# Graph kernel on one core: count scatters among the key gathers, eight buffers for turned blocks, all attribute gathers beside the hops

## The reference, cut to what matters

```python
x = layernorm(x + L0(x))   # 2 transformer layers: attention over edges, then an FFN
x = layernorm(x + L1(x))   # GAT, 4 heads
x = layernorm(x + L2(x))   # hypergraph convolution, twice
x = layernorm(x + L3(x))   # messages from edge_attr_4 and a radial MLP of edge_attr_10

# L0, for each of two layers
scores = einsum('ehd,ehd->eh', q[dst], k[src]) * scale
agg = segment_sum(softmax_by_dst(scores) * v[src], dst)
# L2, for each of two convolutions
m = segment_sum(xt[src], dst) * Binv
out = segment_sum(m[dst], src) * Dinv
# L3
s = node_in[src]; messages = tensor_product(s, edge_attr_4) * radial
agg = segment_sum(messages, dst)
```

## Time and profile before

| | us |
|---|---|
| median of 3 runs | 5292.75 |
| lowest and highest | 5285.0, 5301.71 |
| profiled execution, its own time | 5281.95 |
| its span | 5280.8 |

### The profile page before, as it was taken

One profiled execution on the slowest core, in us unless ns is written; L12 is line 12 of the kernel. 1 busy time (PEld: TensorE's weight loads), 2 busy tenths in 40 slices (PEclk: granted clock), 3 DMA queues, 4 the chain that ended last, 5 costly groups with the idle time before them and its releaser, 6 DMA issues.

```text
span 5280.8 us, 60302 instructions
## 1 busy us (share of the span) xinstructions
PE 3594.7 (68%) x15291; PEld 2666.6 (50%) x15291; DVE 2872.9 (54%) x6726; ACT 1861.5 (35%) x5462; POOL 3684.8 (70%) x3085
## 2 busy tenths in 40 slices
PE   4544444566896444449979705666669999888886
PEld 3433323344564232336646503444458888677876
DVE  6455556888443454578864305666772223334445
ACT  1143334565333343447733201111120100256555
POOL 4466666888887666678888886666687887266664
PEclk9876667899998676669989857888789999889898
DMA  7688887566325898867743225666649899666665
GB/s 258 196 284 273 281 286 218 140 160 135 34 27 140 284 288 288 278 156 166 167 97 26 23 39 149 171 173 167 141 90 285 236 256 261 184 175 176 175 176 143
DMA packets 734946, 951.06 MB, mean 180 GB/s; under 512 B 277381, under 2 KB 526260, under 8 KB 734472
## 3 DMA queue, kind: packets, MB, share of 16 engines
q1 hardware_dynamic: 419634, 538.30, 33.2%
q0 software_dynamic: 298192, 385.84, 31.5%
q10 hardware_dynamic: 16774, 23.00, 1.2%
HBM read 727.03 MB, written 219.80 MB: 179 GB/s over the span
## 4 chain that ended last, share of the span: by engine, by line
PE 32%; issue 23%; DVE 18%; POOL 15%; another core or an unknown queue 5%; DMA 4%; ACT 2%; DVEq 1%; ACTq 0%; POOLq 0%; SPq 0%
PE bank L2657 11%; POOL arena L928 7%; POOL ATT L965 7%; PE bank L2782 6%; PE bank L2362 4%; PE bank L2779 4%; DMA ATT<-arena 3%; DVE arena L1371 3%; DVE arena L1473 2%; DVE arena L1383 2%; DVE arena L1753 2%; PE bank L2564 2%; PE bank L2575 2%; POOL arena L972 2%
## 5 line engine op out<-in xcount | busy, mean ns | idle before, releaser
L928 POOL DMA_INDIRECT arena<-KVT,arena x832 | 802.2, 964 | 479.2 <-issue 272.3
L2497 PE MATMUL bank<-arena 128*128 128x264 f32 x1664 | 600.5, 513 | 660.9 <-issue 322.3
L2497 PEld LDWEIGHTS bank<-arena 128*128 128x128 f32 x1664 | 385.8, 249 | 875.4 <-issue 619.8
L972 POOL DMA_INDIRECT arena<-ATTR,arena x416 | 660.9, 1589 | 155.7 <-issue 155.7
L965 POOL DMA_INDIRECT ATT<-arena x391 | 644.5, 1648 | 124.8 <-issue 109.2
L951 POOL DMA_INDIRECT sc<-arena x391 | 639.2, 1635 | 129.7 <-issue 111.8
L928 POOL DMA_INDIRECT arena<-YT,arena x416 | 406.3, 977 | 299.6 <-issue 105.9
L1473 DVE TENSOR_TENSOR arena<-arena,bank 128x256 f32<-128x256 f32 x832 | 297.2, 411 | 564.8 <-remote 368.1
L928 POOL DMA_INDIRECT arena<-X1T,arena x416 | 414.0, 995 | 249.0 <-issue 129.7
L2454 PE MATMUL bank<-arena 128*128 128x273 f32 x1664 | 454.1, 411 | 141.8 <-DVE arena L1532 94.8
L2270 ACT ACTIVATE arena<-arena 128x128 f32<-128x128 f32 x1248 | 374.9, 387 | 259.1 <-issue 133.4
(11 more groups left out here) (334 smaller groups left out, 6435.7 us busy)
## 6 DMA issues: line engine op xcount, KB each, us to landing
VE<-arena SPq DMA_DIRECT2D x208, 512.0 KB
arena<-VE SPq DMA_DIRECT2D x208, 512.0 KB
left<-ATT SPq DMA_DIRECT2D x250, 320.0 KB
left<-AM SPq DMA_DIRECT2D x250, 320.0 KB
ATT<-arena POOLq DMA_DIRECT2D x25, 1600.0 KB, 6.2
arena<-LOCT SPq DMA_DIRECT2D x312, 128.0 KB
arena<-ATT SPq DMA_DIRECT2D x75, 384.0 KB
AM<-arena SPq DMA_DIRECT2D x100, 256.0 KB
```

Source lines behind the costliest of these rows:

```text
L928: GP.indirect_dma_start(out=ring[:, i % n, k, :], out_offset=None, in_=table, in_offset=bass.IndirectOffsetOnAxis(ap=idx[:, 4 * i + k:4 * ...
L972: GP.indirect_dma_start(out=PA[:, c, 2:6], out_offset=None, in_=ATTR, in_offset=bass.IndirectOffsetOnAxis(ap=PA[:, c, 0:1].bitcast(I), axi ...
L2497: mm = P.matmul(b_[:, 0:264], OHQ[:, i % 3, k * 128:(k + 1) * 128], QS[:, i % 4, k, :], start=True, stop=True)
```

## The change

Three things change.

1. **Counts among the gathers.** A function `count(n)` issues one count scatter. In k0 and k1 one stands behind every second group's gathers, 52 in each stage, 104 in all. The other 287 stay behind k1's gathers. The waits for the places and for the cleared table move ahead of k0's first gather.
2. **Attributes.** The 52 early attribute gathers go; all 416 stand behind l1's gathers, beside the hops, with the wait for `attr_out`.
3. **Eight buffers for turned blocks.** AMT grows from four to eight buffers and moves to the region of the K/V ring (`o_big + 256`). The semaphores `am_out` are dropped; the stores of AM signal the eight semaphores `kept`, of which five are the former `v_kept`.

```diff
-EARLY = 52
+AMRING = 8
@@
-    AMT = view(o_S + 3584, 4, 4, 128)
+    AMT = view(o_big + 256, AMRING, 4, 128)
@@
-    v_kept = [Landed(nc, f"v_kept{k}") for k in range(5)]
+    kept = [Landed(nc, f"kept{k}") for k in range(AMRING)]
+
+    def am_kept(f):
+        k = f % AMRING
+        return kept[k]((2 * len(range(k, G, 5)) if k < 5 else 0) + f // AMRING + 1)
@@
-                                 AMT[:, f % 4, 0:nb, :]).then_inc(am_out[f % 4].sem, 16)
+                                 AMT[:, f % AMRING, 0:nb, :]).then_inc(kept[f % AMRING].sem, 16)
@@
+        def count(n):
+            g, k = n // 4, n % 4
+            c = g + KG * k
+            if g:
+                GP.wait_ge(*counted[k](g))
+            GP.indirect_dma_start(
+                out=ATT, out_offset=bass.IndirectOffsetOnAxis(ap=PLACE[:, c:c + 1], axis=0),
+                in_=ones[:, 0:1], in_offset=None, bounds_check=TABLE - 1,
+                compute_op=ALU.add).then_inc(counted[k].sem, 16)
+
         GP.wait_ge(*index_made("prep", 1))
+        GP.wait_ge(*edges_made("places", 1))
+        GP.wait_ge(*table_clear(PIECES + 1))
@@
-                    GP.wait_ge(*v_kept[i % 5](l * len(range(i % 5, G, 5)) + i // 5))
+                    GP.wait_ge(*kept[i % 5](l * len(range(i % 5, G, 5)) + i // 5))
                 gather(k_, i, KVT, 512, isrc, o_big)
+                if i % 2:
+                    count(l * (G // 2) + i // 2)
@@
-                GP.wait_ge(*edges_made("places", 1))
-                GP.wait_ge(*table_clear(PIECES + 1))
-                for g in range(KG):
-                    for k in range(4):
-                        c = g + KG * k
-                        if c < C:
-...
+                for n in range(2 * (G // 2), C):
+                    count(n)
@@
-        GP.wait_ge(*attr_out(1))
-        add_attributes(range(EARLY))
@@
-        add_attributes(range(EARLY, T))
+        GP.wait_ge(*attr_out(1))
+        for c in range(T):
+...
@@
-            if f >= 4:
-                S.wait_ge(*am_out[f % 4](f // 4))
-            S.activation(AMT[:, f % 4, 0:nb, :], bank[f % 2][:, 0:128 * nb].rearrange("p (b s) -> p b s", s=128),
+            if f >= AMRING:
+                S.wait_ge(*am_kept(f - AMRING))
+            S.activation(AMT[:, f % AMRING, 0:nb, :], bank[f % 2][:, 0:128 * nb].rearrange("p (b s) -> p b s", s=128),
                          ACT.Copy).then_inc(block_copied.sem, 1)
```

More of the change, by code:

```diff
@@ L323, in program @@
     COUNTS = view(o_S, 4, 896)
-    AMT = view(o_S + 3584, 4, 4, 128)
+    AMT = view(o_big + 256, AMRING, 4, 128)
+    assert 256 + AMRING * 512 <= o_ring - o_big
     RS1 = ACC[:, :, 256:260]
@@ L477, in program @@
     left_in = [Landed(nc, f"left_in{k}") for k in range(RIGHT)]
-    am_out = [Landed(nc, f"am_out{k}") for k in range(4)]
     y_out = [Landed(nc, f"y_out{k}") for k in range(4)]
@@ L647, in sync_engine @@
                 SY.wait_ge(*gathered(f"k{l}", i))
-                SY.dma_start(VE[i], KV[:, i % 5, :, 256:512]).then_inc(v_kept[i % 5].sem, 16)
+                SY.dma_start(VE[i], KV[:, i % 5, :, 256:512]).then_inc(kept[i % 5].sem, 16)
                 if i + 6 < G:
@@ L652, in sync_engine @@
             for k in range(5):
-                SY.wait_ge(*v_kept[k]((l + 1) * len(range(k, G, 5))))
+                SY.wait_ge(*kept[k]((l + 1) * len(range(k, G, 5))))
             def load_emb(n):
@@ L780, in sync_engine @@
             if h == 1:
-                for k in range(4):
-                    SY.wait_ge(*am_out[k](2 * W))
+                for f in range(8 * W - AMRING, 8 * W):
+                    SY.wait_ge(*am_kept(f))
             for part in range(5):
@@ L986, in pool_engine @@
             gather("l1", i, X1T, 72, idst, o_ring)
-        add_attributes(range(EARLY, T))
+        GP.wait_ge(*attr_out(1))
+        for c in range(T):
+            GP.indirect_dma_start(
+                out=PA[:, c, 2:6], out_offset=None, in_=ATTR,
+                in_offset=bass.IndirectOffsetOnAxis(ap=PA[:, c, 0:1].bitcast(I), axis=0), bounds_check=R1 - 1,
+                compute_op=ALU.add).then_inc(attr_back.sem, 16)
         GP.wait_ge(*acc_clear("l3", 1))
@@ L1790, in end1 @@
             yield from norm_windows("a0", part)
-        for k in range(4):
-            V.wait_ge(*am_out[k](2 * W))
+        for f in range(8 * W - AMRING, 8 * W):
+            V.wait_ge(*am_kept(f))
         V.wait_ge(*w_landed(W_LOADS["l2"]))
@@ L2081, in scalar_engine @@
             for k in range(5):
-                S.wait_ge(*v_kept[k]((l + 1) * len(range(k, G, 5))))
+                S.wait_ge(*kept[k]((l + 1) * len(range(k, G, 5))))
             copy_scan(f"w{l}", SPs)
```

## The result

The changed kernel took 5335.9 us (median of 4, 5332.35 to 5338.27) beside 5294.03 us for the kernel before (median of 4): ratio 1.0087, 95% interval 1.0074 to 1.0099. The forecast was 5225, the range 5140 to 5345; the time fell into the range's upper end, but the kernel got slower and not faster.

The account below looks back on a forecast made before the run. POOL was taken to bound the stretch before l1, by late counts and early attributes. From the profiled 5281.95 us, -116 + 30 + 0 + 18 gave 5214, plus 10.8 for the median 5225 us; 8-in-10 range 5140 to 5345.

Parts of the forecast that it names:

- additive rival: k0 and k1: ring waits don't shrink, so counts cost 193 us, not 30; 5388 us; chance 0.14 for cost past 114.
- term 1: Stretch before l1: 104 counts and all 52 early attributes leave it, so l1 starts earlier, -116 us.
- Term 2: k0 and k1: 52 counts among each stage's gathers partly fill POOL's ring waits, +30 us for both stages.
- The held-up landings: k0 and k1: each count delays the landing of a group's gathers, 378 us in place of 30; 5573 us; chance 0.05.
- The ring that pays: l1 and key stages: half of DVE's 88.6 us wait goes and key stages cost 0; 5151 us; chance 0.15.
- the gap: Before l1: something behind POOL holds l1 back, so the 116 us gain is halved; 5283 us; chance 0.05.
- the deciding point: k0 and k1: from a cost of 98 us for both stages together, slower POOL time decides the outcome.
- Term 3: l1: eight buffers for turned blocks change nothing, since four were rarely short; 0 us, bound up to -89.
- Term 4: Beside the hops: 52 more attributes outlast the 82.06 us slack, so l3 starts later, +18 us.
- The median: Whole kernel: 10.8 us added at the end, since the median lay that far above the profiled run.

Follow-up runs that it names:

- second run: The whole changed kernel measured once more, against the kernel before: 5293.9 us beside 5263.7, ratio 1.0053.
- experiment 10: Kernel before with 104 indirect adding reads among the key gathers, all counts behind k1: 5390.6 us beside 5266.9, ratio 1.0239.
- 11: Kernel before with no attributes ahead of l1 and 12 counts ahead of k0's wait for source indices: 5165.2 us beside 5266.9, ratio 0.9812.
- experiment 3: Kernel before with the eight buffers for turned blocks alone: 4874.4 us beside 4879.5, ratio 0.9993.

## Why the prediction was wrong

The total lies inside the stated range, but that is no credit to the forecast: the range reached up to 5345 for the additive rival's sake, and the change was to be a gain.

**What bounds the kernel, term 1: right.** The stretch from k1 to l1 gave back 119 us, 116 forecast. The clearing of the accumulator (3173.95 + 5.89 = 3179.8) was what came last and POOL's gather followed at 3181.4. PE hid the 287 counts. DVE's first step of l1 came 10.9 us behind that gather (3192.26) and not 6.3: the first counts load took 5.3 us to reach PE (3183.08 to 3188.38), where the forecast had 3.6.

**Term 2, the counts among the gathers: wrong, and it turned the sign.** It was put at 30 us for both stages and measured 151 (133 in the second run). The step that failed is the overlap: counts that fill POOL's ring waits leave 14 us, and 30 was taken from there. It treats a count as 1.86 us of POOL's time and the ring wait as room for it. Half of that was right. Work of POOL does fill the waits: 98 us of memsets cost nothing, until POOL goes back to back. But a count is not only work of POOL. In the slow condition the scores come 16 to 19 us behind the landings; with more indirect DMAs that lag grows (in k1 16.1 us before, 17.5 after, 20.5 with 104 plain reads), and a key stage takes close to 1.5 us for every indirect DMA in it, however long POOL issues it:

| k1, slow condition | indirect DMAs | us | us per DMA |
|---|---|---|---|
| before, first trace | 416 | 621.1 | 1.49 |
| V store cut, 29% fewer bytes per us | 416 | 622.2 | 1.50 |
| 54 us of filler | 416 | 608.8 | 1.46 |
| 98 us of filler (POOL alone needs 618) | 416 | 622.4 | 1.50 |
| after | 468 | 700.0 | 1.50 |
| after, second run | 468 | 689.6 | 1.47 |
| reads of 1.86 us | 468 | 690.7 | 1.48 |
| plain reads of 1.25 us | 520 | 770.2 | 1.48 |

52 more at 1.5 are 78 us per stage, 156 for both, against the measured 151. That agreement is in part luck: one more indirect DMA cost 1.36 and 1.55 us in the first pair of traces (k0, k1), 1.26 and 1.30 in the second, 1.23 and 1.28 as a read of 1.86 us (experiment 10 against 11, timed side by side), and 1.43 as a plain read. What the runs show is that this price doesn't follow POOL's time (1.86 us for a count, 1.25 for a plain read), and that filler of POOL's time alone has no price up to 618 us. A fixed limit of 1.5 us per DMA they don't show: the smaller filler came to 1.46. The other view of DMA load in that term, 0.42 us of 16 engines per count, was +44 us for both stages; the DMA share fell from 0.86 and 0.89 to 0.82 and 0.83, so those engines were not the limit.

**The rivals.** The additive one had the right side and the wrong reason: in the slow condition POOL's time is free until POOL goes back to back, and the counts cost 151 and not 193. It had the scores follow each landing at a fixed distance; in k1 the distance is 2.7 us in the quick condition, and before it runs from a few up to 25 us. In the quick condition, where POOL never waits, its price is the true one (99 + 102 us). The held-up landings are refuted by the landings themselves, which were known no later than before (5.8 us against 5.9 in k1). The ring that pays did not, and the gap did close. I gave 0.14 to the additive rival's band; the deciding point, 98 us for both stages, was worked out rightly and was passed.

**What I could have read.** In the earlier trace rows and the windows the stage's length divided by its gathers was 1.52 and 1.49 us, where POOL issues in 1.25; l3's gathers took 623.8 us, again 1.50 each (l1's took 662.7, 1.59). And the trace of before already had the scores 16 to 18 us behind the V stores, with the nameless waits of DVE between them: the waits that I counted as POOL's slack were the far side of a delay in PE, DVE and ACT, and no row told what that delay would do with one more DMA.

**Term 3, the ring: right** (0 forecast, -2 measured). **Term 4, attributes beside the hops: right in the slow condition** (16 of 18 us), and 33 in the quick one, where the hops end sooner.

**The median:** the 10.8 us between profiled run and median were 3.6 in the changed kernel (5332.35 and 5335.9).

**What stays open:** what delays PE, DVE and ACT in the slow condition, why more indirect DMAs delay them more, and why the condition comes and goes. The runs show where it is felt (waits of DVE for products, up to 10 us, with no releaser to be seen) and that a pause of 2 us in POOL's issuing behind every second group nearly does away with it (3.2 us from V store to scores); a pause of 1.1 us only lessens it (12.5). In these pauses POOL also waits for its own memset, which it doesn't for a count, and no version tells the two apart. In k1 the granted TensorE clock is not it: between its two levels of 0.5 and 1.0 it averaged 0.69 before and 0.77 in experiment 3, but PE was busy for 293.0 and 295.7 us, so its work took equally long and the difference is idling. In l1 and l3 the clock can have a part: 0.78 and 0.89 before, 0.87 and 0.99 in experiment 3, with PE busy for 23 and 49 us more in stages that took 114 and 70 us more. The runs don't show the resource.

## What to carry to other kernels

Before you put work into an engine's waits, ask what the wait is made of. Two readings tell: when the data's landing is known, and how far behind it the step comes that frees the buffer. Here the landings were on time and the scores 16 us behind them, so the side behind the landing set the pace, and work of POOL was free only if it didn't slow that side. Then try a filler of the same length but another kind: POOL's waits had room for memsets and not for one more indirect DMA. In such a stage the number of indirect DMAs is what has to fall, and more of them belong where nothing else gathers (here POOL's wait of 26 to 31 us ahead of the first key gather, and the stretches beside dense work).

## What the runs showed of the hardware that I had not expected

- In the slow condition the key stages took 1.46 to 1.52 us for each indirect DMA of 128 pieces in them, when those of 4-byte pieces are counted like those of 2 KB, though POOL issues a gather in 1.25 us; in the quick condition, without counts, k1 took 523.0/416 = 1.26.
- The same kernel took 4880 us at one time and 5285 at another on the same chip. The gather stages make the difference (k0 535 or 635, l1 549 or 662, l3 553 or 623 us); the order scatters, at 1.95 us each, took 764 and 761.
- That difference isn't in the gathers' landing but behind it: in k1 the landing was known 5.9 us behind the last gather in both, and the scores were made 2.7 us behind that in one and 16.1 in the other.
- 48 memsets of POOL with 1.1 us each, put between gathers, left k1 at 608.8 us, 12 to 13 us shorter than without them.
